# Four graph layers on one core: pair loops written out, and a wait for GpSimd in layer 1

## The chip, the core and the metric

The kernel runs on one core of one Trainium2 chip. The metric is the device time of one execution in microseconds (us). A core has five engines with queues of their own: TensorE (PE; its weight loads are PEld), VectorE (DVE), ScalarE (ACT), GpSimd (POOL) and SyncE (SP), which only issues DMAs here. They meet through semaphores.

## The reference

64 graphs of 128 nodes with 256 features pass through four layers. After each there is a layer norm of x plus the layer's output:

```
x = _layernorm(x + _L0_gnn_ref(x, adj, ...))   # hypergraph convolution, 256 -> 512 -> 256
x = _layernorm(x + _L1_gnn_ref(x, adj, ...))   # attention weights
x = _layernorm(x + _L2_gnn_ref(x, adj, ...))   # three-step random walk
x = _layernorm(x + _L3_gnn_ref(x, adj, ...))   # tanh attention
```

Layer 1, with which much of what follows deals, is

```
q, k = jnp.split(jnp.einsum('bnd,ed->bne', x, W_qk), 2, axis=-1)
v = jnp.einsum('bnd,ed->bne', x, W_v)
scores = jnp.einsum('bnd,bmd->bnm', q, k) * inv_scale
w = jax.nn.softmax(jnp.sum(scores * adj_matrix, axis=-1, keepdims=True), axis=1)
return w * v
```

## The kernel before

Four graphs are a group (GP = 4), so there are 16 groups (G). A layer is a pipeline of steps, one per group; `step(g, p, has)` issues the work of one step on one engine, with p the parity of the buffers and `has(k)` true if group g + k exists. Each engine walks layers 1 to 3 with `over_layers` (L81 on): steps up to 3 are written out with constants, steps 4 to 13 are five passes of a `Fori` over pairs of groups, in which each wait's value and many addresses are computed from a register, and the last steps are written out again, interleaved with the first of the next layer. SyncE's program is already written out (`unrolled=True`). Layer 0 has a loop of its own (`over_groups`) that the change leaves alone. `wait_ge(sem, upto(g, per, k))` waits for k pieces of group g when each group makes `per` of them; `reused(g, back)` is false only for a constant g below `back`.

Numbers are kept as pairs of float16 tiles, hi and lo. `triple` (L105) makes one exact product of three matmuls (L110 to L112). For the next groups x has to be split and transposed:
- ScalarE writes the high half, `x_high` (L1118), two groups ahead.
- GpSimd subtracts to make the low half, `x_low` (L1125): two SBUF inputs, 128x1024, once per group. It waits for the high half and for the buffer.
- SyncE's `transpose_x` (L1139) issues a DMA transpose for each half into xT_hi and xT_lo, high half first, low half when `x_low` is done. Behind it in layer 1 SyncE copies a group of adjT (`stage_adj`, L1181), and comes to the next group's high half.
- TensorE waits for both in `transposed`.

Layer 1, step by step and by engine, in program order:
- TensorE: `aggregate(g-1)` (L1213, fp32), `project(g, 0)` and `(g, 1)` (24 products of 384 columns per group, L110 to L112), `score_rows(g-1)` (L1221, the transpose of the score sums), `project(g, 2)` and `(g, 3)`, `weight_columns(g-1)` (L1225).
- ScalarE: `x_high(g+2)`, `norm_apply(g-2)` four times (L1073), `exponentials(g)` (L1256), `copy_qkv(g+1)` four times (L1250).
- VectorE: `weights(g-1)` (L1282), `residual(g-1)` four times (L1288: l_pre from l_vqk, a column and x_resident, 128x256), two statistics (L1039), `scores(g)` (L1296, L1297, L1302), two statistics, `maximum(g)` (L1306, L1310), `norm_variance(g-1)` (L1046 and on), `softmax(g)` (L1314, L1318).
- GpSimd: `x_low(g+2)`, then `norm_scales(g-1)` (L1058 to L1067), which begins with a wait for the four statistics.

A residual increments the semaphore `L.pre_ok`, four per group. The two loops over the weight columns and the residuals make a cycle: scores of g need the copies of g, the weights need the scores, the residuals the weights.

In layer 2 a TensorE step ends and begins with `walk_mid` (L1513 is its bias matmul), which waits for halves that ScalarE and VectorE have just made from PSUM; `node_scores(g+1)` then waits for xT of group g+1. In layer 3 VectorE's residuals (L1901) read PSUM and SBUF.

Of the kernel before, what the change touches and what calls it, by code (L numbers as in the profile page):

```python
# [12 lines left out]
GP = 4  # L13
# [9 lines left out]
TURNS_PE = ((2, True), (2, True))  # L23
TURNS_ACT = ((2, True), (0, True))
TURNS_DVE = ((2, True), (2, True))
TURNS_POOL = ((2, True), (2, True))
# [11 lines left out]
def upto(g, per, k):  # L38

    return g * per + k  # L40
# [36 lines left out]
def over_layers(eng, programs, turns, unrolled=False):  # L77

    before, drain, after, ahead = None, 0, 2, True
    for (step, lead, lag), (until, next_ahead) in zip(programs, turns + ((2, True),)):
        first = 4 if lag else 2
        for g in range(-2, first):
            for which in ((step, before) if ahead else (before, step)):
                if which is step and g >= -lead:
                    step(g, g % 2, lambda k, g=g: 0 <= g + k < G)
                if which is before and before and G + g + after < G + drain:
                    i = G + g + after  # L90
                    before(i, i % 2, lambda k, i=i: 0 <= i + k < G)
        if not unrolled:
            with eng.Fori(first // 2, G // 2 - 1) as pair:
                step(pair * 2, 0, lambda k: True)
                step(pair * 2 + 1, 1, lambda k: True)
        for g in range(first if unrolled else G - 2, G - 2 + until):
            step(g, g % 2, lambda k, g=g: 0 <= g + k < G)
        before, drain, after, ahead = step, lag, until, next_ahead
    for g in range(G, G + drain):
        before(g, g % 2, lambda k, g=g: g + k < G)  # L100


def reused(g, back=2):

    return not isinstance(g, int) or g >= back  # L105


def triple(nc, out, lhs, rhs, start=True, stop=True, **kw):

    nc.tensor.matmul(out, lhs[0], rhs[1], start=start, stop=False, **kw)  # L110
    nc.tensor.matmul(out, lhs[1], rhs[0], start=False, stop=False, **kw)  # L111
    return nc.tensor.matmul(out, lhs[0], rhs[0], start=False, stop=stop, **kw)  # L112
# [49 lines left out]
def graph_layers(nc, K):  # L162

    with ExitStack() as ctx:
        K.x_new, K.scores_after = {}, {}
        second = layer2(nc, K, ctx)
        with ExitStack() as tiles:
            layers = [layer1(nc, K, ctx, tiles), second]
        layers.append(layer3(nc, K, ctx))
        with nc.Block() as block:  # L170
            @block.sync
            def _(sp):
                over_layers(sp, [sync(sp) for sync, _, _, _, _ in layers], TURNS_SP, unrolled=True)
                sp.wait_ge(K.stored, 16 * (G - 1 + GP))

            @block.tensor
            def _(pe):
                over_layers(pe, [tensor(pe) for _, tensor, _, _, _ in layers], TURNS_PE)

            @block.scalar  # L180
            def _(act):
                over_layers(act, [scalar(act) for _, _, scalar, _, _ in layers], TURNS_ACT)

            @block.vector
            def _(dve):
                over_layers(dve, [vector(dve) for _, _, _, vector, _ in layers], TURNS_DVE)

            @block.gpsimd
            def _(pool):
                over_layers(pool, [gpsimd(pool) for _, _, _, _, gpsimd in layers], TURNS_POOL)  # L190


def setup(nc, K, ctx, W1, b1, gamma, beta, W2, b2, W_qk, W_v, Wv, bv, aw, ab, Wk, bk, w3, a3):
# [900 lines left out]
def front_of(shared, layer):  # L1094
    F = Parts()
    F.x_hi, F.x_lo, F.xT_in, F.xs, F.xT = shared.x_hi, shared.x_lo, shared.xT_in, shared.xs, shared.xT
    F.base = (layer - 1) * G
    F.made = 2
    F.ahead = 2 if layer < 3 else 0
    return F  # L1100
# [7 lines left out]
def x_group(K, g):  # L1108

    return K.x[:, xcols(g - G if isinstance(g, int) and g >= G else g)].rearrange("p (g d) -> p g d", g=GP)  # L1110
# [10 lines left out]
def x_low(K, F, pool, g, p):  # L1121
    pool.wait_ge(F.x_hi, upto(F.base + g, 1, 1))
    if reused(F.base + g):
        transposed(F, pool, g - 2, p)
    pool.tensor_tensor(F.xs[p][1], x_group(K, g), F.xs[p][0], ALU.subtract).then_inc(F.x_lo, 1)  # L1125


def transposed(F, eng, g, p):

    eng.wait_ge(F.xT_in[p], 16 * (F.base + g - p) + 32)  # L1130
# [12 lines left out]
def layer1(nc, K, ctx, tiles):  # L1143
# [10 lines left out]
    L = norm(nc, ctx, "l1", tiles=tiles)  # L1154
# [16 lines left out]
    F = front_of(K.F, 1)  # L1171
# [21 lines left out]
    def tensor(pe):  # L1193
        def project(g, p, j):
            if j == 0:
                transposed(F, pe, g, p)
            if reused(g, 1):
                pe.wait_ge(qkv_sb, upto(g - 1, GP, j + 1))
            for d in range(DT):
                m = triple(nc, b_qkv[j][:, 0:2 * QK + D], [s[:, j, d, :] for s in F.xT[p]],  # L1200
                           [w[:, d, :] for w in K.qkv], start=d == 0, stop=d == DT - 1)
            m.then_inc(qkv_ps, 1)

        def aggregate(g, p):
            pe.wait_ge(a_in[p], 8 * (g - p) + 16)
            pe.wait_ge(qkv_sb, upto(g, GP, GP))
            if isinstance(g, int) and g == 0:
                pe.wait_ge(k_one, 2)
            if reused(g):
                pe.wait_ge(asum_ok, upto(g - 2, 1, 1))  # L1210
                pe.wait_ge(qa_ok, upto(g - 2, 1, 1))
            for j in range(GP):
                m = pe.matmul(b_as[p][:, j * (QK + 1):(j + 1) * (QK + 1)], ast[p][:, j * N:(j + 1) * N],  # L1213
                              vqk[p][:, j, D + QK:D + 2 * QK + 1], start=True, stop=True)
            m.then_inc(ak_ps, 1)

        def score_rows(g, p):
            pe.wait_ge(w_ok, upto(g, 1, 1))
            if reused(g):
                pe.wait_ge(wgt_ok, upto(g - 2, 1, 1))  # L1220
            pe.transpose(b_as[p][0:GP, rows], w[p][:], K.ident[:]).then_inc(wT_ps, 1)  # L1221

        def weight_columns(g, p):
            pe.wait_ge(wn_ok, upto(g, 1, 1))
            pe.matmul(b_as[p][:, cols], wn[p][:], K.ident[0:GP, 0:GP], start=True,  # L1225
                      stop=True).then_inc(wB_ps, 1)

        def step(g, p, has):
            q = 1 - p
            if has(-1):  # L1230
                aggregate(g - 1, q)
            if has(0):
                project(g, p, 0)
                project(g, p, 1)
            if has(-1):
                score_rows(g - 1, q)
            if has(0):
                project(g, p, 2)
                project(g, p, 3)
            if has(-1):  # L1240
                weight_columns(g - 1, q)
        return step, 0, 1

    def scalar(act):
        def copy_qkv(g, p, j):
            act.wait_ge(qkv_ps, upto(g, GP, j + 1))
            if reused(g):
                act.wait_ge(ak_ps, upto(g - 2, 1, 1))
                act.wait_ge(L.pre_ok, upto(g - 2, GP, j + 1))
            act.activation(vqk[p][:, j, 0:D + 2 * QK], b_qkv[j][:, 0:2 * QK + D], ACT.Copy).then_inc(qkv_sb, 1)  # L1250

        def exponentials(g, p):
            act.wait_ge(wneg_ok, upto(g, 1, 1))
            if reused(g):
                act.wait_ge(wn_ok, upto(g - 2, 1, 1))
            act.activation(wexp[p][:], b_as[p][0:GP, rows], ACT.Exp, bias=wneg[p][:], scale=SC,  # L1256
                           accum_out=wsum[p][:]).then_inc(wexp_ok, 1)

        def step(g, p, has):
            q = 1 - p  # L1260
            if halves_due(F, g + 2):
                x_high(K, F, L, act, g + 2, p)
            if has(-2):
                norm_apply(K, L, act, g - 2, p, 0)
                norm_apply(K, L, act, g - 2, p, 1)
                norm_apply(K, L, act, g - 2, p, 2)
                norm_apply(K, L, act, g - 2, p, 3)
            if has(0):
                exponentials(g, p)
            if has(1):  # L1270
                copy_qkv(g + 1, q, 0)
                copy_qkv(g + 1, q, 1)
                copy_qkv(g + 1, q, 2)
                copy_qkv(g + 1, q, 3)
        return step, 2, 2
# [68 lines left out]
        return step, 0, 1  # L1344

    def gpsimd(pool):
        def step(g, p, has):
            q = 1 - p
            if halves_due(F, g + 2):
                x_low(K, F, pool, g + 2, p)  # L1350
            if has(-1):
                norm_scales(K, L, pool, g - 1, q)
        return step, 2, 1
# [611 lines left out]
```

## Time and profile before

| | |
|---|---|
| median of 3 runs | 776.5 us (774.9 to 778.07) |
| the profiled execution | 778.61 us, of which the span of its instructions is 776.8 us |
| TensorE | busy 696.9 us (90%), 5654 matmuls |
| VectorE | busy 588.0 us (76%) |
| ScalarE | busy 531.9 us (68%) |
| GpSimd | busy 343.3 us (44%) |
| mean granted clock of TensorE | 0.948 |
| layer 0, 1, 2, 3 | to about 303, 303 to 446, 446 to 660, 660 to 777 us |
| instruction transfers | 28 of 16 KB on queue q8, 28 of up to 8 KB on q14 |

The profile is one execution. A row of the timeline gives start and duration in us, the engine, the source line, the operation, the tiles that it writes and reads, a count when several are merged (the duration is then from the start of the first to the end of the last), and in brackets the idle time before it with what ended it. A tile's name leaves out buffer numbers. The granted clock is a share of 2.4 GHz.

### The profile page before, as it was taken

Reading aid. Unit: us, or ns where it says so; the run is one execution under the profiler, and the core shown is the slowest. Engines: PE = TensorE matmul, PEld = TensorE weight load, DVE = VectorE, ACT = ScalarE, POOL = GpSimd, SP = SyncE. Lnnn points to the kernel's source line nnn. Section 1 sums busy time; section 2 is a strip of 40 time slices with the busy share of each in tenths; the row PEclk is TensorE's granted clock in tenths of the full one; section 3 lists DMA queues with packets and bytes.
Section 4 is the critical chain, followed back from the end, with each engine's and each line's share of the span. In section 5 each row is a group of like instructions: output and inputs, shape, how many; then the busy total and the mean of one; then the engine's idle time right before and its main releaser. Section 6 shows DMA issues by size and latency. Waiting matters only on the chain.

```text
span 776.8 us, 18723 instructions
## 1 busy us (share of the span) xinstructions
PE 696.9 (90%) x5654; PEld 504.1 (65%) x5654; DVE 588.0 (76%) x1744; ACT 531.9 (68%) x1177; POOL 343.3 (44%) x418
## 2 busy tenths in 40 slices
PE   5899999999999985777878589899989998999995
PEld 5677777777777753444445366566666666888874
DVE  4888888888878762777887876767676876588995
ACT  4668887767777763465555557667776776688885
POOL 2243455434344451444444425243524253677773
PEclk9999999999999997997797689999999999799998
DMA  9522032232221020643444334634343333266663
GB/s 285 154 84 70 29 109 69 73 117 83 68 68 54 2 53 30 149 83 81 95 89 100 55 55 82 83 77 87 81 82 81 81 73 65 55 164 162 162 145 128
DMA packets 168144, 71.11 MB, mean 92 GB/s; under 512 B 122260, under 2 KB 165654, under 8 KB 168088
## 3 DMA queue, kind: packets, MB, share of 16 engines
q1 hardware_dynamic: 166496, 70.41, 37.8%
q8 instruction: 28, 0.46, 0.3%
q10 hardware_dynamic: 1592, 0.01, 0.1%
q14 instruction: 28, 0.23, 0.1%
HBM read 28.46 MB, written 8.39 MB: 47 GB/s over the span
## 4 chain that ended last, share of the span: by engine, by line
PE 39%; DVE 8%; issue 6%; DMA 4%; ACT 2%; SPq 1%; DVEq 1%; POOL 0%; ACTq 0%; POOLq 0%
PE bank L110 10%; PE bank L112 10%; PE bank L111 10%; DMA xT_lo<-x_halves 4%; PE bank L1804 3%; DVE l_pre L1288 2%; DVE l_st L1039 2%; PE bank L1407 2%; PE bank L1802 1%; SPq L1139 1%; PE bank L1225 1%; PE bank L1513 1%; DVE l_w L1302 1%; DVE l_qa L1296 1%; ACT x_resident L1073 1%
## 5 line engine op out<-in xcount | busy, mean ns | idle before, releaser
L1073 ACT ACTIVATE x_resident<-l_pre,l_nmr,l_rstd 128x256 f32 (+1 forms) x256 | 136.9, 595 | 26.8 <-POOL l_nmr L1067 26.7
L1125 POOL TENSOR_TENSOR x_halves<-x_resident,x_halves 128x1024 f16<-128x1024 f16 (+1 forms) x46 | 100.1, 2176 | 39.2 <-ACT x_halves L1118 37.1
L110 PE MATMUL bank<-Wk_lo,xT_hi 128*128 128x2 f16 (+2 forms) x384 | 94.0, 274 | 4.8 <-DMA xT_lo<-x_halves 4.8
L1039 DVE BATCH_NORM_STATS2 l_st<-l_pre 128x6 f32<-128x256 f32 x256 | 96.5, 413 | 1.1
L111 PE MATMUL bank<-Wk_hi,xT_lo 128*128 128x2 f16 (+2 forms) x384 | 95.1, 273 | 0.0
L112 PE MATMUL bank<-Wk_hi,xT_hi 128*128 128x2 f16 (+2 forms) x384 | 94.7, 272 | 0.0
L983 POOL TENSOR_TENSOR hq<-hq 128x512 f32<-128x512 f32 x32 | 43.1, 1347 | 76.6 <-ACT hq L716 76.6
L1064 POOL TENSOR_TENSOR l_rstd<-l_veps,minus_half 128x4 f32<-128x4 f32 x64 | 64.6, 1009 | 24.1 <-DVE l_veps L1053 22.7
L110 PE MATMUL bank<-W2T_lo,h_hi 128*128 128x257 f16 x256 | 70.7, 276 | 2.3 <-DVE h_lo L860 1.2
L111 PE MATMUL bank<-W2T_hi,h_lo 128*128 128x257 f16 x256 | 70.8, 277 | 0.0
L112 PE MATMUL bank<-W2T_hi,h_hi 128*128 128x257 f16 x256 | 70.8, 276 | 0.0
L1729 POOL TENSOR_TENSOR l_T_lo<-l_tf,l_T_hi 128x512 f16<-128x512 f32 x16 | 18.5, 1157 | 106.6 <-ACT l_T_hi L1573 106.6
L860 DVE TENSOR_TENSOR h_lo<-hf,h_hi 128x512 f16<-128x512 f32 x64 | 44.7, 702 | 18.9 <-ACT hf L705 8.3
L1288 DVE SCALAR_TENSOR_TENSOR l_pre<-l_vqk,l_wgt,x_resident 128x256 f32<-128x256 f32 x64 | 55.0, 922 | 1.9 <-DVE l_wgt L1282 1.7
L722 ACT ACTIVATE zf<-bank 128x258 f32<-128x258 f32 x64 | 24.7, 388 | 46.2 <-PE bank L637 46.1
L705 ACT ACTIVATE hf<-bank,b_col 128x512 f32<-128x512 f32 x64 | 44.0, 687 | 16.1 <-PE bank L112 15.6
L110 PE MATMUL bank<-qkvT_lo,xT_hi 128*128 128x384 f16 x128 | 48.0, 375 | 6.2 <-PEq L527 6.2
L110 PE MATMUL bank<-xT_lo,W1T_hi 128*128 128x512 f16 x128 | 48.5, 379 | 1.6 <-DVE qkvT_lo L414 1.5
L112 PE MATMUL bank<-xT_hi,W1T_hi 128*128 128x512 f16 x128 | 48.5, 379 | 0.0
L111 PE MATMUL bank<-xT_hi,W1T_lo 128*128 128x512 f16 x128 | 48.5, 379 | 0.0
L1118 ACT ACTIVATE x_halves<-x_resident 128x1024 f16 (+1 forms) x46 | 48.4, 1052 | 0.0
L971 POOL TENSOR_TENSOR zrs<-zvar,minus_half 128x4 f32<-128x4 f32 x16 | 22.0, 1378 | 59.0 <-DVE zvar L897 59.0
(206 smaller groups left out, 2119.6 us busy)
## 6 DMA issues: line engine op xcount, KB each, us to landing
adj<-in_adj SPq DMA_DIRECT2D x32, 256.0 KB, 3.7
x_halves<-in_x SPq DMA_DIRECT2D x16, 512.0 KB, 3.7
x_resident<-in_x SPq DMA_DIRECT2D x16, 512.0 KB, 4.8
out<-x_resident SPq DMA_DIRECT2D x15, 512.0 KB, 3.2
l_adjT<-adjT_resident SPq DMA_DIRECT2D x16, 256.0 KB, 2.5
x_resident<-in_L_gnn_W SPq DMA_DIRECT2D x2, 512.0 KB, 5.7
x_resident<-in_L_gnn_Wk SPq DMA_DIRECT2D x1, 768.0 KB, 8.1
xT_hi<-x_halves SPq DMA_TRANSPOSE x48, 3.2
```

What stands on the lines that cost most here:

```text
L110: nc.tensor.matmul(out, lhs[0], rhs[1], start=start, stop=False, **kw)
L111: nc.tensor.matmul(out, lhs[1], rhs[0], start=False, stop=False, **kw)
L112: return nc.tensor.matmul(out, lhs[0], rhs[0], start=False, stop=stop, **kw)
L705: act.activation(hf[:, h, :], b_hid[h % 2][:], ACT.Relu, bias=K.b1[:, h:h + 1], scale=1.0 / W_SCALE).then_inc(hf_ok, 1)
L860: dve.tensor_tensor(hs[1][:, h, :], hf[:, h, :], hs[0][:, h, :], ALU.subtract).then_inc(h_lo, 1)
L983: pool.tensor_tensor((hqs if h == HT - 1 else hq[:, 0, :])[:], hq[:, 0, :], hq[:, h, :], ALU.add).then_inc(hqs_ok, 1)
L1039: dve.bn_stats(L.st[p][:, j, :], L.pre[p][:, j, :]).then_inc(L.st_ok, 1)
L1064: pool.tensor_tensor(L.rstd[p][:], L.veps[p][:], K.minus_half[:], ALU.pow).then_inc(L.rstd_ok, 1)
L1073: act.activation(K.x[:, gcols(g, j)], L.pre[p][:, j, :], ACT.Identity, bias=L.nmr[p][:, j:j + 1], scale=L.rstd[p][:, j:j + 1]).then_inc(L. ...
L1118: act.activation(F.xs[p][0], x_group(K, g), ACT.Copy).then_inc(F.x_hi, 1)
L1125: pool.tensor_tensor(F.xs[p][1], x_group(K, g), F.xs[p][0], ALU.subtract).then_inc(F.x_lo, 1)
L1288: dve.scalar_tensor_tensor(L.pre[p][:, j, :], vqk[p][:, j, 0:D], wgt[p][:, j:j + 1], K.x[:, gcols(g, j)], ALU.mult, ALU.add).then_inc(L.pr ...
```

## The change

TensorE, ScalarE, VectorE and GpSimd also get `unrolled=True`: `over_layers` leaves out the `Fori` and calls `step` for every group, in the same order, with constants in all waits and addresses. And in layer 1 GpSimd's low half of group g+2 waits, from the fourth group on, until all four residuals of group g-1 are done. The order of GpSimd's work doesn't change.

```
 def over_layers(eng, programs, turns, unrolled=False):
...
         if not unrolled:
             with eng.Fori(first // 2, G // 2 - 1) as pair:
                 step(pair * 2, 0, lambda k: True)
                 step(pair * 2 + 1, 1, lambda k: True)
         for g in range(first if unrolled else G - 2, G - 2 + until):
             step(g, g % 2, lambda k, g=g: 0 <= g + k < G)
```

```diff
             @block.tensor
             def _(pe):
-                over_layers(pe, [tensor(pe) for _, tensor, _, _, _ in layers], TURNS_PE)
+                over_layers(pe, [tensor(pe) for _, tensor, _, _, _ in layers], TURNS_PE, unrolled=True)
...
             @block.scalar
             def _(act):
-                over_layers(act, [scalar(act) for _, _, scalar, _, _ in layers], TURNS_ACT)
+                over_layers(act, [scalar(act) for _, _, scalar, _, _ in layers], TURNS_ACT, unrolled=True)
...
             @block.vector
             def _(dve):
-                over_layers(dve, [vector(dve) for _, _, _, vector, _ in layers], TURNS_DVE)
+                over_layers(dve, [vector(dve) for _, _, _, vector, _ in layers], TURNS_DVE, unrolled=True)
...
             @block.gpsimd
             def _(pool):
-                over_layers(pool, [gpsimd(pool) for _, _, _, _, gpsimd in layers], TURNS_POOL)
+                over_layers(pool, [gpsimd(pool) for _, _, _, _, gpsimd in layers], TURNS_POOL, unrolled=True)
...
     def gpsimd(pool):
+        def low_half(g, p):
+            if reused(g, 3):
+                pool.wait_ge(L.pre_ok, upto(g - 3, GP, GP))
+            x_low(K, F, pool, g, p)
+
         def step(g, p, has):
             q = 1 - p
             if halves_due(F, g + 2):
-                x_low(K, F, pool, g + 2, p)
+                low_half(g + 2, p)
             if has(-1):
                 norm_scales(K, L, pool, g - 1, q)
```

## Rows read from the trace of the kernel before

**Rows 1.** Windows: start:end, length, busy us per engine, granted clock, DMA share, GB/s.

```profile
302.60:343.90 41.30, 30.78 (x185) 18.85 (x185) 28.10 (x80) 20.63 (x46) 15.63 (x17) 0.95 0.50 112
343.90:439.50 95.60, 76.86 (x373) 45.67 (x373) 74.55 (x215) 54.10 (x121) 41.95 (x55) 0.80 0.39 85
453.10:657.90 204.80, 192.98 (x1700) 132.09 (x1698) 149.09 (x462) 143.97 (x363) 80.49 (x96) 1.00 0.42 80
668.10:770.60 102.50, 99.16 (x1048) 81.76 (x1045) 85.97 (x276) 83.81 (x203) 70.76 (x89) 1.00 0.57 139
```

**Rows 2.** The chain that ended last, in layer 1: start, us, what.

```profile
322.86 0.95 DVE l_pre L1288 x3
324.26 2.10 issue
```

**Rows 3.** VectorE's residuals of layer 1: two groups of the timeline, durations in ns.

```profile
L1288 DVE SCALAR_TENSOR_TENSOR l_pre<-l_vqk,l_wgt,x_resident x64: 472/481/2399, 315.0 to 445.7; 128x256 f32<-128x256 f32 x64
322.86 3.59 DVE L1288 SCALAR_TENSOR_TENSOR l_pre<-l_vqk,l_wgt,x_resident 128x256 f32<-128x256 f32 x4
444.55 1.67 DVE L1288 SCALAR_TENSOR_TENSOR l_pre<-l_vqk,l_wgt,x_resident 128x256 f32<-128x256 f32 x4
```

**Rows 4.** Timeline of a step of layer 1 that is written out already.

```profile
323.11 1.08 PE L1213 MATMUL bank<-l_vqk,l_adjT 128*128 128x65 f32 x8 [0.49 <-issue]
324.04 2.13 POOL L1125 TENSOR_TENSOR x_halves<-x_resident,x_halves 128x1024 f16<-128x1024 f32 x1 [1.10 <-ACT x_halves L1118]
327.94 0.08 PEld L1221 LDWEIGHTS bank<-ident,l_w 128*4 128x4 f32 x1 [2.19 <-DVE l_w L1302]
327.94 0.27 PE L1221 MATMUL bank<-ident,l_w 128*4 128x128 f32 x1 [1.80 <-DVE l_w L1302]
328.83 0.14 DVE L1046 TENSOR_TENSOR l_mdiff<-l_st 128x4 f32<-128x4 f32 x1
330.09 0.38 PE L1225 MATMUL bank<-ident,l_wn 4*128 4x4 f32 x2
330.70 0.88 DVE L1288 SCALAR_TENSOR_TENSOR l_pre<-l_vqk,l_wgt,x_resident 128x256 f32<-128x256 f32 x2
```

**Rows 5.** Timeline of layer 3 under a low half of GpSimd.

```profile
697.01 2.13 POOL L1125 TENSOR_TENSOR x_halves<-x_resident,x_halves 128x1024 f16<-128x1024 f16 x1
697.58 0.74 DVE L1039 BATCH_NORM_STATS2 l_st<-l_pre 128x6 f32<-128x256 f32 x2
698.36 0.81 DVE L1046 TENSOR_TENSOR l_mdiff<-l_st 128x4 f32<-128x4 f32 x1
```

**Rows 6.** Tile xT_lo: in 320:440, in 486.3:492; and TensorE's waits in 455:655.

```profile
L1139 SPq DMA_TRANSPOSE xT_lo<-x_halves x14: 1232/1232/1310, 326.2 to 440.0; - x14
DMA to landing us min/median/max: 3.1/3.1/3.2
...
DMA to landing us min/median/max: 4.7/4.7/4.7
...
PE bank L110 <- DMA xT_lo<-x_halves: 4.8, 4, 1.7
```

**Rows 7.** Timeline of TensorE's bias matmuls in layer 2, first of a step.

```profile
474.10 0.27 PE L1513 MATMUL bank<-bk_parts,ones 128*128 128x256 f16 x1
486.39 0.27 PE L1513 MATMUL bank<-bk_parts,ones 128*128 128x256 f16 x1
...
526.91 0.27 PE L1513 MATMUL bank<-bk_parts,ones 128*128 128x256 f16 x1 [0.36 <-DVE l_mid_lo L1685]
...
551.95 0.27 PE L1513 MATMUL bank<-bk_parts,ones 128*128 128x256 f16 x1 [0.36 <-DVE l_mid_lo L1685]
```

**Rows 8.** DMA queues (packets, MB, share) in 454:518, 518:642 and 668:697.

```profile
q8 instruction: 5, 0.08, 0.6%
...
q8 instruction: 1, 0.02, 0.0%
...
q8 instruction: 2, 0.03, 0.6%
```

## The prediction

> **What bounds the kernel now.** I began with the windows of layers 1 to 3 [rows 1]. In layers 2 and 3 TensorE is busy for 193.0 of 204.8 us and 99.2 of 102.5 us at the full clock, so these layers are TensorE's. Layer 1 is another case: in its first 41.3 us TensorE is busy for 30.8, and from 343.9 to 439.5 the mean granted clock is 0.80. The clock has two levels, 1.0 and 0.5 (2.4 and 1.2 GHz), so 0.80 means that 0.4 of this stretch, 38 us, ran at half clock.
>
> The chain through layer 1 says who sets its step [rows 2]: three residuals of a group on VectorE, then 2.10 us of "issue" before it goes on; behind that it runs through the statistics, the scores, TensorE, and the next group's residuals. The "issue" is explained by the rows of the residual [rows 3]: four instructions take 3.59 us at 322.86, and the single instruction's spread is 472/481/2399 ns. The last group's four, beside which GpSimd has no low half to make, take 1.67 us. At 322.86 GpSimd's subtraction of 2.13 us (the low half of x, group g+2) starts at 324.04, in the middle [rows 4]. One residual per group waits until it ends. The price is 3.59 - 1.67 = 1.92 us a step, on the chain, and TensorE idles for 1.80 us before the transpose of the scores [rows 4].
>
> The first residual starts at 315.0 and the last group's first at 444.55 [rows 3]: 15 steps in 129.5 us, 8.63 each. A step ahead of the loop, at full clock, is 7.84 us (322.86 to 330.70 [rows 3, 4]). So 0.79 us a step goes to register work in the loop and to half clock, and 1.92 us of the rest to GpSimd's subtraction.
>
> **The low half of layer 1 waits for the residuals.** No work is added, one wait per step is. The subtraction of group g+2 now starts behind the fourth residual of group g-1. Set t = 0 at the first residual. The four end at 1.67, so the subtraction runs from about 1.75 to 3.88. What does VectorE do then? Four statistics, the product of scores (one operand in PSUM), a reduction, the maximum (PSUM) and the negation (one tiny operand). The first instruction with two SBUF operands, l_mdiff, starts 2.38 us behind the end of the residuals (328.83 less 326.45 [rows 3, 4]), so at 4.05, when the subtraction is over. Does the subtraction hold what runs meanwhile? Layer 3 shows it: under GpSimd's subtraction from 697.01 to 699.14 two statistics take 0.74 us, which is what two take anywhere, while the l_mdiff behind them lasts 0.81 us instead of 0.14 to 0.16, until the subtraction is over [rows 5]. So I count the hold as gone and not moved: step 7.84 - 1.92 = 5.92.
>
> What comes late next? Two other rings run through the step, and I price each. **TensorE's own ring:** the step of 7.85 us less the wait for the scores, which the weight load puts at 2.19 and the matmul, whose end is modelled late, at 1.80 [rows 4]: 5.66 to 6.05, I take 5.9. In it are a wait of 0.49 for ScalarE's copies ahead of the aggregation and about 0.3 ahead of the weight columns. **The transposed low half:** the subtraction ends at 3.88, SyncE issues at once (the old subtraction ends at 326.17, the issue starts at 326.2), and the data lands 3.1 us later, at 7.0 [rows 4, 6]. The projection of group g+2, one step on, needs it: twelve matmuls stand before the next transpose of scores, some 1.95 us (as many, and the transpose, fit in the 2.15 us from 327.94 to 330.09), and 2.76 us pass from there to the residuals (327.94 to 330.70 [rows 4]). That is 11.7 us for two steps, 5.9 for one. Queued behind the late low half on SyncE are the copy of adjT (issued at 5.1 instead of 4.6, needed a step and more later) and the next high half (due at 6.9, free by 5.8). Behind the new wait on GpSimd stand the norm's scales of group g-1, which wait for statistics that end at 4.0 anyhow. So three rings meet at 5.9 us; nothing has slack, and anything late shows.
>
> On this point the Trainium skill (SBUF — State Buffer, Who interferes with whom) says that a VectorE instruction with at most one SBUF input keeps clear of GpSimd unless it is in a two-port mode, and counts tensor_scalar among those that can enter one. The trace agrees on the statistics; the negation, a tensor_scalar right ahead of l_mdiff, would by that rule be held if the subtraction ran later than I have it. By this count 0.1 us is between them, so the rule gives 0 here, and a few tenths a step if the start slips; the sum doesn't need it.
>
> **The clock.** It fell behind 41.3 us in which TensorE was busy for 75%, with a piece of idling of 1.80 us in every step [rows 1, 4]. With the step at 5.92, 0.8 us of idling is left in pieces of 0.3 to 0.5, a busy share of some 87%; layer 2, at 94%, kept the full clock for 204.8 us. 87 is nearer to 94 and its pieces are short, so I take the clock as full. If it isn't, the 5.1 busy us of a step double; this is a rival below.
>
> **The loops written out.** Gone are 15 loop passes of two groups, with their register arithmetic before waits. In layer 1 this is counted already, since 7.84 is a step ahead of the loop. In layer 2 two written-out steps are 12.29 apart (474.10 to 486.39), two looped ones 25.04 (526.91 to 551.95), 12.52 each, with 0.36 us of idling before walk_mid's bias matmul [rows 7]. Ten steps: 10 x 0.23 = 2.3 us saved. In layer 3 TensorE idles for 3.3 us in all [rows 1]; I take 0.5 saved, with bounds of 0 and 2.
>
> **What is added is code.** The page of DMA queues has a line for instruction transfers: q8 carries 16 KB pages. From 454 to 518 (layer 2, written out) there are five, from 518 to 642 (looped) one; from 668 to 697 (layer 3, written out) two [rows 8]. Does a page cost anything? The transpose of a low half issued at 486.3 shares its flight with one, and lands after 4.7 us instead of 3.1. In layer 2 TensorE waits four times for such a low half, 4.8 us in all, 1.7 at most [rows 6]: three waits of about 1.5, behind 486, 500 and 577, and a small one. Two of the five pages written out hit, and the one of the loop. So: layer 2 gets about 9 more pages, of ten in all two fifths hit, 4 x 1.5 = 6.0, less the 1.5 that the one cost: +4.5. Layer 3 gets 4 to 5 more; transposes are in flight for more than half of its step, but no wait of the kind in layer 2 is in its rows, so I take half and 0.5 each: +1.2. Layer 1 gets 4 more; half hit, at 1.2: +2.4. Bounds: none hits (-1.5, since the one of before may go) and all hit (+1.5 x 18 = +27).
>
> The Trainium skill (Runtime: NRT & Kernel Launch, Instruction fetch mechanics) holds that streaming in straight-line code is mostly hidden and that a taken branch is what breaks it. By that the 8.1 us above would be 0 and the time about 733. The trace shows the other side, the transfer that the page delays; the engine's own fetching cost nothing that I can see.
>
> **Sum**, against the profiled run's 778.6 us (span 776.8):
> - layer 1: 15 x (8.63 - 5.92) = -40.7, pages +2.4: -38.3
> - layer 2: -2.3 + 4.5 = +2.2
> - layer 3: -0.5 + 1.2 = +0.7
> - the turn to layer 2 ran at half clock (439.5 to 453.1) and is bound by dependences; 0, with a bound of -2.
>
> This is -35.4, or 743.2 us. The profiled run lies 2.1 above the median of 776.5, so 741.
>
> **Rivals.**
> - *The clock keeps falling in layer 1.* For: three rings without slack, pieces of idling in each step. Against: busy share nearer to layer 2's. With the old share of half clock (0.4) and a step of 10.2 at half clock (2 x 5.1), the mean step is 1/(0.6/5.92 + 0.4/10.2) = 7.1, layer 1 costs 106.5 instead of 88.8: 741 + 17.7 = 759.
> - *Code pages hit nearly always.* For: transposes are in flight much of every step. Against: two of five. All hits: +27 instead of 8.1, 760.
> - *The hold only moves (the change does not do what it says, and is slower).* GpSimd's subtraction at its new place holds statistics or scores as it held the residual. Then the step stays 8.63 with half clock as before, layer 1 saves the loop's register work alone, 2.3 as in layer 2, and pages cost 2.4 + 4.5 + 1.2 against 2.3 + 0.5: 776.5 - 2.3 + 8.1 - 2.8 = 779.5, and 783.5 when pages hit half again as often: slower. It decides from a hold at the new place of the full 1.9 us a step on. Against it: 0.74 for the two statistics [rows 5].
>
> **Chances.** Forecast (731 to 752) 0.79; clock 0.11; pages 0.06; hold moved 0.04, of which half within 0.5% and half above. The range takes the forecast with bounds: no page hit and the turn at full clock, 731, and on the other side the clock falling in most of the old places, 758. What a measurement can tell here is about 0.5% (3.9 us). Faster 0.96, same 0.02, slower 0.02.
>
> **What would show it.** Four residuals in 1.67 us; the subtraction starting 0.1 us behind them; first residuals 5.9 to 6.1 us apart; granted clock 1.00 from 306 to the end of layer 1; score transpose no longer waiting 1.8 us; q8 pages up from the 28 of the page of before to some 45, and TensorE waiting for xT_lo more often in layer 2. I am wrong if statistics above 0.41 us appear in layer 1, if the step is above 6.5, or if half-clock stretches remain.

## The result

The changed kernel takes 736.5 us (median of 4 runs, 735.6 to 737.1); the kernel before, beside it, 777.3 us. The ratio is 0.947, with a 95% interval of 0.943 to 0.951. Forecast were 741 us, with a range of 731 to 758. Its profiled execution took 737.1 us with a span of 735.2.

In the tables of this document a layer lasts from the first residual of its first group to the first residual of its last group, by the timeline of VectorE; between layers stand the turns.

| us | to layer 1 | layer 1 | turn | layer 2 | turn | layer 3 | end | span |
|---|---|---|---|---|---|---|---|---|
| before | 315.1 | 129.5 | 19.1 | 189.2 | 14.5 | 99.9 | 9.5 | 776.8 |
| after | 316.6 | 90.3 | 18.5 | 186.0 | 11.9 | 102.6 | 9.3 | 735.2 |
| difference | +1.5 | -39.2 | -0.6 | -3.1 | -2.6 | +2.7 | -0.2 | -41.6 |

The 1.5 us ahead of layer 1, where the code is the same, is what two executions differ by; this place was between 313.2 and 316.3 in the runs below.

**Windows of the changed kernel** (start:end, length, busy us per engine with counts, granted clock, DMA share, GB/s): layer 1, 2 and 3.

```profile
308.20:403.80 95.60, 85.45 (x546) 54.73 (x544) 76.62 (x297) 73.00 (x165) 55.43 (x72) 1.00 0.62 129
414.10:615.40 201.30, 193.63 (x1715) 131.65 (x1713) 154.21 (x463) 143.79 (x364) 82.11 (x95) 1.00 0.43 82
618.90:725.00 106.10, 100.64 (x1087) 84.19 (x1085) 73.98 (x270) 87.09 (x211) 72.53 (x89) 1.00 0.59 136
```

Against [rows 1]: the mean clock of layer 1 is 1.00 where 343.9 to 439.5 had 0.80, and TensorE is busy for 85.5 of 95.6 us instead of 76.9, part of which was at half clock. The 15 steps take 90.3 us instead of 129.5; the clock goes to a half at 403.8, in the last 3.0 us of the layer.

**Layer 1's step in the changed kernel**, first the line of the residual (ns: min/median/max), then the timeline (start, us, instruction, and in brackets the idle time ahead and its end).

```profile
L1288 DVE SCALAR_TENSOR_TENSOR l_pre<-l_vqk,l_wgt,x_resident x64: 474/479/486, 316.5 to 408.0; 128x256 f32<-128x256 f32 x64
```

```profile
347.10 1.67 DVE L1288 SCALAR_TENSOR_TENSOR l_pre<-l_vqk,l_wgt,x_resident 128x256 f32<-128x256 f32 x4
347.36 1.08 PE L1213 MATMUL bank<-l_vqk,l_adjT 128*128 128x65 f32 x8 [0.49 <-issue]
348.69 0.75 DVE L1039 BATCH_NORM_STATS2 l_st<-l_pre 128x6 f32<-128x256 f32 x2
348.85 2.13 POOL L1125 TENSOR_TENSOR x_halves<-x_resident,x_halves 128x1024 f16<-128x1024 f32 x1 [1.66 <-DVE l_pre L1288]
349.35 0.41 DVE L1296 TENSOR_TENSOR l_qa<-bank,l_vqk 128x256 f32<-128x256 f32 x1
349.80 0.42 DVE L1302 TENSOR_REDUCE l_w<-l_qa 128x4 f32<-128x256 f32 x1
350.13 0.74 DVE L1039 BATCH_NORM_STATS2 l_st<-l_pre 128x6 f32<-128x256 f32 x2
350.27 0.27 PE L1221 MATMUL bank<-ident,l_w 128*4 128x128 f32 x1
...
351.01 1.23 SPq L1139 DMA_TRANSPOSE xT_lo<-x_halves  x1
351.09 0.14 DVE L1310 TENSOR_SCALAR l_wneg<-l_wmax 4x1 f32<-4x1 f32 x1
351.16 0.14 DVE L1046 TENSOR_TENSOR l_mdiff<-l_st 128x4 f32<-128x4 f32 x1
352.42 0.29 PEld L1225 LDWEIGHTS bank<-ident,l_wn 4*128 4x128 f32 x2 [0.32 <-DVE l_wn L1318]
```

Compare with [rows 3] and [rows 4]. No residual of the 64 is longer than 0.486 us; before, 15 took 2.34 to 2.40. The subtraction starts 0.08 us behind the residuals (GpSimd idled 1.66 us ahead of it, up to l_pre) and ends at 350.98. Beside it lie two statistics of 0.75, the scores, the reduction and two more statistics of 0.74, none longer than without it; the negation comes at 351.09, 0.11 us behind. TensorE's transpose of the scores no longer has a bracket of 1.80. The idling shown is the 0.49 of TensorE and the 0.32 us of its weight load. From here to the next step's first residual (353.04) it is 5.94 us.

**Waits of TensorE in the changed kernel's layer 2** (waiting instruction, releaser, us, times, longest).

```profile
PE bank L110 <- DMA xT_lo<-x_halves: 3.1, 4, 1.3
PE bank L1518 <- ACT l_mid_hi L1572: 1.1, 3, 0.5
```

The same view of its layer 3:

```profile
PE bank L110 <- DMA xT_lo<-x_halves: 4.9, 7, 1.0
```

Before, these waits were 4.8 us in 4 times in layer 2 [rows 6] and 0.5 us in one time in layer 3.

**The DMA queues that carry code, changed kernel** (q8 the 16 KB pages, q14 the 8 KB pages), between the residuals of the first and the last group (packets, MB, share of the 16 engines), layer 2:

```profile
q8 instruction: 13, 0.21, 0.5%
q14 instruction: 12, 0.10, 0.2%
```

and layer 3:

```profile
q8 instruction: 9, 0.15, 0.6%
q14 instruction: 6, 0.05, 0.1%
```

Before, layer 2 had 6 on q8 and 8 on q14, layer 3 had 4 and 3. In the whole kernel q8 went from 28 to 42; forecast were some 45.

### The profile page after: what moved, and what is told of

The parts are those of the page before. It is cut to its first block, busy times and chain, and to the rows that moved or that the text cites. A ratio compares the mean times of both kernels' runs of the same rounds, so it can differ in the third digit from the quotient of the medians.

```text
span 735.2 us, 17541 instructions
## 1 busy us (share of the span) xinstructions
PE 676.4 (92%) x5654; PEld 494.2 (67%) x5654; DVE 554.1 (75%) x1744; ACT 529.9 (72%) x1177; POOL 343.5 (47%) x418
## 4 chain that ended last, share of the span: by engine, by line
PE 36%; DMA 11%; SPq 3%; DVE 3%; issue 2%; POOL 1%; ACT 1%; ACTq 0%; POOLq 0%; DVEq 0%
PE bank L110 11%; DMA xT_lo<-x_halves 11%; PE bank L112 10%; PE bank L111 10%; SPq L1139 3%; PE bank L1213 1%; PE bank L1412 1%; POOL x_halves L1125 1%; DVE l_st L1039 1%; PE bank L1518 1%; DVE l_pre L1288 1%; PE bank L1225 1%; ACT l_mid_hi L1572 0%; DVE l_lr L1652 0%; PE bank L1809 0%
## 5 line engine op out<-in xcount | busy, mean ns | idle before, releaser
L1073 ACT ACTIVATE x_resident<-l_pre,l_nmr,l_rstd 128x256 f32<-128x256 f32 (+1 forms) x256 | 137.1, 598 | 16.6 <-POOL l_nmr L1067 16.6
L1125 POOL TENSOR_TENSOR x_halves<-x_resident,x_halves 128x1024 f16<-128x1024 f32 x46 | 100.9, 2193 | 38.0 <-DVE l_pre L1288 28.0
L110 PE MATMUL bank<-w_lo,xT_hi 128*128 128x1 f16 (+1 forms) x256 | 45.5, 221 | 5.5 <-DMA xT_lo<-x_halves 4.9
L110 PE MATMUL bank<-qkvT_lo,xT_hi 128*128 128x384 f16 x128 | 42.6, 333 | 7.1 <-PEq L527 6.2
L1118 ACT ACTIVATE x_halves<-x_resident 128x1024 f16<-128x1024 f32 x46 | 48.4, 1051 | 0.0
```

The costliest lines, as they stand in the source:

```text
L1073: act.activation(K.x[:, gcols(g, j)], L.pre[p][:, j, :], ACT.Identity, bias=L.nmr[p][:, j:j + 1], scale=L.rstd[p][:, j:j + 1]).then_inc(L. ...
L1118: act.activation(F.xs[p][0], x_group(K, g), ACT.Copy).then_inc(F.x_hi, 1)
```

## Experiments

Each is a small edit of the changed kernel. The times are medians (of 4 executions; 2 for e8, 6 for e11 and e12, 8 for e7), with the ratio to executions of the kernel before made beside them. The layers are those of one profiled execution each.

| kernel | us | ratio (95%) | layer 1 | layer 2 | layer 3 |
|---|---|---|---|---|---|
| e1_unroll_only | 764.3 | 0.982 (0.979 to 0.986) | 117.9 | 190.4 | 101.9 |
| e2_wait_only | 739.3 | 0.952 (0.947 to 0.957) | 92.3 | 189.3 | 98.8 |
| e3_l3_looped | 733.7 | 0.943 (0.939 to 0.946) | 90.1 | 186.4 | 100.1 |
| e4_l3_pe_looped | 732.7 | 0.943 (0.939 to 0.947) | 90.0 | 185.6 | 101.0 |
| e5_wait_three | 735.3 | 0.945 (0.938 to 0.952) | 90.2 | 186.0 | 102.3 |
| e6_wait_two | 745.2 | 0.959 (0.953 to 0.965) | 97.5 | 188.6 | 101.3 |
| e7_unroll_delay | 777.1 | 0.996 (0.992 to 1.000) | 132.1 | 188.6 | 99.3 |
| e8_low_memset | 736.2 | 0.947 (0.938 to 0.956) | 89.2 | 186.3 | 101.6 |
| e9_order | 749.7 | 0.962 (0.958 to 0.966) | 104.6 | 186.7 | 101.5 |
| e10_order_three | 743.8 | 0.958 (0.952 to 0.962) | 95.0 | 188.9 | 102.4 |
| e11_order_l3_pe_looped | 743.1 | 0.953 (0.950 to 0.957) | 98.0 | 188.2 | 100.7 |
| e12_pe_l1_only | 733.6 | 0.946 (0.943 to 0.950) | 90.0 | 185.3 | 100.5 |

### One half of the change at a time

e1_unroll_only drops the wait:

```diff
         def low_half(g, p):
-            if reused(g, 3):
-                pool.wait_ge(L.pre_ok, upto(g - 3, GP, GP))
             x_low(K, F, pool, g, p)
```

> The loops written out, without the new wait. My theory: GpSimd's subtraction holds one residual per step again (four in 3.59 us, the longest single one about 2.4), TensorE idles 1.8 us before the scores' transpose and the clock falls as before. A step of layer 1 at full clock takes 7.84 us, the 15 steps about 127 us instead of 90.3, and the kernel about 772 us. Rival, that writing out is what shortens layer 1: 15 steps near 90 us and a time below 745 us.

In e1_unroll_only, the line of the residual (ns: min/median/max):

```profile
L1288 DVE SCALAR_TENSOR_TENSOR l_pre<-l_vqk,l_wgt,x_resident x64: 478/481/2405, 313.2 to 432.2; 128x256 f32<-128x256 f32 x64
```

Its window of layer 1:

```profile
304.90:427.80 122.90, 86.37 (x545) 54.40 (x543) 104.87 (x297) 73.21 (x165) 56.98 (x72) 1.00 0.48 102
```

The transpose of the scores in its timeline of TensorE:

```profile
341.79 0.27 PE L1221 MATMUL bank<-ident,l_w 128*4 128x128 f32 x1 [1.81 <-DVE l_w L1302]
```

The hold is back (2.405), the step is 7.86 in 11 of the 15 cases, and TensorE idles 1.81 us. But the clock stays full up to 427.8, 3 us before the layer ends: 117.9 us, not the 127 that I expected, and 764.3 us where I expected 772. So writing out alone saves 11.6 us in layer 1, far more than its register work, and the wait then saves 27.6, which is 1.84 a step.

e2_wait_only keeps the wait and takes `unrolled=True` from the four engines:

```diff
-                over_layers(pe, [...], TURNS_PE, unrolled=True)
+                over_layers(pe, [...], TURNS_PE)
```

(and the same for ScalarE, VectorE and GpSimd.)

> The new wait alone, the loops of TensorE, ScalarE, VectorE and GpSimd kept. My theory: four residuals in 1.67 us, written-out steps of layer 1 at 5.93 us, looped ones 0.25 longer (6.2), 15 steps in about 92.5 us, full clock; layers 2 and 3 as in the kernel before (189 and 100 us); the kernel at about 740 us. Rival, that registers in the loop stand in all three rings of layer 1, now that none has slack: looped steps of 6.5 us or more and 744 us or more.

Its window of layer 1:

```profile
306.30:405.30 99.00, 87.45 (x549) 55.65 (x547) 77.33 (x300) 73.40 (x165) 56.44 (x73) 1.00 0.59 125
```

As expected: no residual above 0.486 us, looped steps 6.15 to 6.25 but for one of 6.75 (behind a wait of 0.75 for a low half), 92.3 us in layer 1, full clock in this window. The wait alone gives 38 of the 41 us. The two halves overlap: 11.6 and 37.2 us, but 39.2 together, since with either of them alone the falls of the clock were gone.

### What makes the clock fall

In e1 TensorE idled 1.81 us in each step and was busy for 86.4 of 122.9 us, 70%, and the clock stayed full. The kernel before and e1 differ little up to the first fall: from the clock's rise at 306.3 to its fall at 343.9 TensorE was busy for 27.7 of 37.6 us before, 73.6%, and in the same stretch of e1 (304.9 to 341.6) for 27.1 of 36.7, 73.9%. The fall at 343.9 came in the first looped steps, right behind an idle piece of 2.04 us. e7_unroll_delay puts a fill of 0.22 us a step on the chain of e1, without any loop:

```diff
             if has(0):
+                dve.memset(idle[:], 0.0)      # idle: 128x192, read by nobody
                 scores(g, p)
```

> The loops written out without the new wait, with a fill of 128x192 on VectorE ahead of the scores of layer 1 in each step (0.2 us, an unused tile). Without the fill the step is 7.86 and the clock is full through layer 1, though TensorE idles in one piece of 1.8 us; in the loops of the kernel before, with 2.03, it fell again and again. If the length of that idling tips the clock, the fill brings the falls back: steps of 8.05 at full clock and some of 9 and more, 15 steps of 125 us or above. If it is something in the loop itself, the clock stays full and 15 steps take 121 us.

The fill in its timeline of VectorE:

```profile
356.85 0.22 DVE L1335 MEMSET l_idle<- 128x192 f32 x1
```

Its window of layer 1:

```profile
316.20:448.30 132.10, 102.77 (x509) 61.85 (x510) 107.67 (x316) 70.39 (x158) 56.84 (x75) 0.79 0.43 92
```

The falls are back: mean clock 0.79, steps of 7.97 to 8.07 between others of 9.0 to 9.7, 132.1 us. At full clock a step is 8.03, 0.17 above e1's, so 15 fills add 2.6 us; they cost 14.2 in the profiled executions and 12.8 by the medians of the kernels. (The profiled execution is the slowest of eight; the fastest took 770.9 us, 6.9 above the fastest of e1.) Falls like those of the loop thus come without a loop, from a few tenths of idling more. They began at once: the first three steps are 9.65, 9.59 and 9.08, and the clock fell at 321.5, right behind an idle piece of 2.05 us.

### Is it the reading that holds the residual

e8_low_memset is e1 with another instruction in GpSimd's place (the low half of x is zero in the products of layer 1 and of layer 2's first two groups; the waits of `x_low` are kept):

```diff
-            pool.tensor_tensor(F.xs[p][1], x_group(K, g), F.xs[p][0], ALU.subtract).then_inc(F.x_lo, 1)
+            pool.memset(F.xs[p][1], 0.0).then_inc(F.x_lo, 1)
```

> The loops written out without the new wait; GpSimd fills the low half of x with zeros in layer 1 instead of subtracting, so the low part of x is missing in the products of layer 1 and of the first two groups of layer 2. The fill starts where the subtraction did, amid the residuals, but reads nothing from SBUF. If the hold comes from the reading of two engines, no residual is held: 0.48 us each, and the step is 5.9 us without the new wait; the low half is also ready over 2 us sooner, so if the step is still 5.9, the ring through the transposes isn't what sets it. Rival, that any work of GpSimd holds the residual: the step is 7.86 less what the fill is shorter.

Its timeline of VectorE and, in the second fence, of GpSimd in one step:

```profile
332.06 1.67 DVE L1288 SCALAR_TENSOR_TENSOR l_pre<-l_vqk,l_wgt,x_resident 128x256 f32<-128x256 f32 x4
```

```profile
333.23 0.95 POOL L1351 MEMSET x_halves<- 128x1024 f16 x1 [1.07 <-ACT x_halves L1118]
```

The fill starts in the midst of the residuals, 0.03 us ahead of the fourth, where e1's subtraction started 0.01 ahead of it, and the four take 1.67 us all the same. So it is not GpSimd's being at work, but its reading from SBUF while VectorE wants two operands from there. The step is 5.94, though the low half is ready 1.8 us sooner than in the changed kernel (2.12 instead of 3.88 us behind the first residual): the ring through the transposes does not set the 5.93.

e6_wait_two and e5_wait_three change the count that is waited for (to 2, and to 3 in e5_wait_three):

```diff
-                pool.wait_ge(L.pre_ok, upto(g - 3, GP, GP))
+                pool.wait_ge(L.pre_ok, upto(g - 3, GP, 2))
```

> The changed kernel, with the low half waiting for two of the four residuals. If the hold comes from the shared way to SBUF and is decided by who starts first, the third residual is on its way and the fourth is held until the subtraction ends: one residual of about 2.0 to 2.4 us per step, a step of 7.5 to 7.9 us, the kernel at 760 to 764 us, like without the wait. Rival, that the start of the subtraction and not the overlap matters: 5.93 us and 736.

> The changed kernel, with the low half waiting for three of the four residuals. It asks what sets the step of 5.93 us. The subtraction can start some 0.4 us earlier, beside the fourth residual. If GpSimd then waits until the fourth is done, or the fourth has read already, nothing is held and the ring through the transposed low half is shorter by up to 0.2 us a step: if that ring sets the step, it falls to 5.75 and the kernel to 733.5 us; if TensorE's or VectorE's ring does, it stays 5.93 and 736. Rival: the fourth residual is held like in the kernel before (2.4 us), the step is near 7.8 and the kernel near 764.

Two steps of e6_wait_two, in the timelines of VectorE (residuals) and, in the second fence, of GpSimd (subtractions):

```profile
333.76 1.67 DVE L1288 SCALAR_TENSOR_TENSOR l_pre<-l_vqk,l_wgt,x_resident 128x256 f32<-128x256 f32 x4
342.24 3.55 DVE L1288 SCALAR_TENSOR_TENSOR l_pre<-l_vqk,l_wgt,x_resident 128x256 f32<-128x256 f32 x4
```

```profile
335.00 2.42 POOL L1125 TENSOR_TENSOR x_halves<-x_resident,x_halves 128x1024 f16<-128x1024 f32 x1 [1.16 <-DVE l_pre L1288]
343.30 2.21 POOL L1125 TENSOR_TENSOR x_halves<-x_resident,x_halves 128x1024 f16<-128x1024 f32 x1 [1.16 <-DVE l_pre L1288]
```

The fourth residual by itself in these two steps:

```profile
334.95 0.48 DVE L1288 SCALAR_TENSOR_TENSOR l_pre<-l_vqk,l_wgt,x_resident 128x256 f32<-128x256 f32 x1
343.43 2.36 DVE L1288 SCALAR_TENSOR_TENSOR l_pre<-l_vqk,l_wgt,x_resident 128x256 f32<-128x256 f32 x1
```

I expected a hold in every step or in none. It came in three of 15, each a step of 7.81, and which it is goes by who starts first. In these three the subtraction starts 0.13 to 0.14 us ahead of the fourth residual (343.30 against 343.43), and the residual lasts 2.35 to 2.36 us. In the other twelve it starts 0.04 to 0.05 us behind it (335.00 against 334.95), the residual takes its 0.48, and the subtraction lasts 2.42 to 2.43 instead of 2.13: now GpSimd is the one that waits. Where the two started within 0.01 us of each other, as in most steps of e1, it was always the residual that was held. The wait for two is not what sets the subtraction's start, though the bracket names the residual: ScalarE's high half ends 0.13 to 0.14 us ahead of it in all 15 steps, and the second residual ended before that. The step of 8.48 us, the one between the two shown, has no hold: TensorE waited 0.73 us for a low half in it, and the clock was at a half from 336.1 to 339.5.

With three, GpSimd's span was 2.30 to 2.31 in all steps and no residual was held; undisturbed steps stayed at 5.93 to 5.94, as expected if the rings of TensorE and VectorE set them. The wait for all four keeps the residuals clear of the subtraction wherever ScalarE's work ends, and costs nothing.

### Can the step be made shorter

e9_order shortens the rings of TensorE and VectorE in layer 1 (VectorE's part in short):

```diff
             if has(0):
                 project(g, p, 0)
+            if has(-1):
+                aggregate(g - 1, q)            # was ahead of project(g, p, 0)
+            if has(0):
                 project(g, p, 1)
...
-            stats 0, 1; scores(g); stats 2, 3; maximum(g); norm_variance(g - 1); softmax(g)
+            scores(g); stats 0, 1; maximum(g); stats 2, 3; softmax(g); norm_variance(g - 1)
```

> The changed kernel with another order in layer 1: TensorE aggregates behind the first projection (it no longer waits 0.49 us for ScalarE's copies), VectorE makes the scores ahead of the statistics, the maximum behind two of them, the softmax ahead of the variance. The rings of TensorE and VectorE get shorter, to about 5.45 and 5.5 us by the rows. If these set the step of 5.93, it falls to what the ring through the transposed low half allows, which I put at 5.87 (two steps in 11.7): 15 steps in 88 to 89 us, the kernel at 734 to 735. Rival, that something shorter binds in neither: 5.5 us a step and 730.

One projection in its timeline of TensorE:

```profile
345.64 0.39 PE L110 MATMUL bank<-qkvT_lo,xT_hi 128*128 128x384 f16 x1 [1.90 <-DMA xT_lo<-x_halves]
```

TensorE's waits in its layer 1:

```profile
PE bank L110 <- DMA xT_lo<-x_halves: 13.7, 7, 2.7
```

Windows of its layer 1, and of the stretch from the clock's rise to its first fall:

```profile
315.70:420.30 104.60, 87.74 (x513) 56.48 (x514) 77.07 (x301) 70.91 (x158) 57.71 (x74) 0.89 0.52 116
308.20:318.50 10.30, 8.76 (x58) 5.70 (x57) 3.56 (x12) 5.22 (x11) 3.15 (x2) 1.00 0.45 106
```

It is 13 us slower than the changed kernel, where 1.5 to 2.5 us less were expected. Every second group TensorE waits 1.9 us for the low half, and steps alternate, 5.42 and 8.9, or 5.42 and 7.4 in the two pairs in which the clock stayed full. The two short rings reach 5.42, so they, one or both, had set the 5.93. The third ring spans two steps, and I had moved the aggregation and the scores into it: they now stand behind the projection that waits for the transposes. The sum of two steps is 12.8 at full clock, not 11.7. The rest of the loss goes with the clock: 23.3 us of the layer ran at half clock, against 3.0 in the changed kernel. It first fell at 318.5, after 10.3 us in which TensorE was busy for 85%, and 1.5 us behind an idle piece of 1.54 us.

e10_order_three adds the wait for three, e11_order_l3_pe_looped also TensorE's loop in layer 3:

> The same order, with the low half waiting for three residuals. With three the subtraction of the low half ended 0.2 to 0.3 us earlier, and the ring through it spans two steps: a step 0.1 to 0.15 below that of the kernel with the order alone, about 5.75 us, 15 steps in 87 us, the kernel at 733 to 734, if that ring binds there; no difference if it does not. A risk: subtraction and fourth residual start closer together, and a held residual costs 1.9 us in its step.

> The order and the wait for three, and TensorE's loop kept in layer 3 (five q8 pages fewer there). If the gains add up: layer 1 in 87 us and layer 3 in 100 to 101 us, the kernel at 730 to 731 us. If pages in layer 3 do not matter, it is that of the same kernel with layer 3 written out.

In e10 two steps are 7.04 and 5.5, 12.6 together, 0.12 a step below e9's 12.8 at full clock: that the low half comes a little earlier does count, as expected, because in this order that ring binds. But that is about 2 of the 9.6 us between 104.6 and 95.0. The rest goes with the clock: 3.9 us of e10's layer 1 ran at half clock and 23.3 of e9's. e11 has the same code in layer 1 as e10, with 10.3 us at half clock and 98.0 us. The level of 87 us was off for both, and so were the times: neither is under 90.3 in layer 1, and layer 3's gain (100.7) doesn't make up for it.

### What the written-out code costs

e3_l3_looped keeps the `Fori` in layer 3 on all four engines, e4_l3_pe_looped on TensorE alone (SyncE is written out everywhere, as before):

```diff
-        for g in range(first if unrolled else G - 2, G - 2 + until):
+        for g in range(first if written else G - 2, G - 2 + until):   # written: per layer
...
-                over_layers(pe, [...], TURNS_PE, unrolled=True)
+                over_layers(pe, [...], TURNS_PE, unrolled=(True, True, False))
```

> The changed kernel with layer 3 in its loop again on all four engines. My theory: layer 3 lost 2.7 us by being written out (99.9 to 102.6 us from the first to the last group's residuals), because pages of code delay its transposes; looped, it is back at about 100 us and the kernel at 734 us, with one or two q8 pages in layer 3 instead of eight. Rival, that the loss is not from pages but from another timing of the engines at the start of the layer: layer 3 stays at 102 us or more, the kernel at 736.5.

> The changed kernel with layer 3 in its loop again on TensorE alone. If the 16 KB pages of queue q8 are TensorE's and these are what delays the transposes, q8 has no page in the looped stretch and layer 3 takes about 100 us, as with all four engines looped (734 us). If the 8 KB pages of the other engines count as much, layer 3 stays between 101 and 102.6 us and the kernel at 735.5 us or more.

TensorE's waits in layer 3 of e3_l3_looped, which the changed kernel has at 4.9 us in 7 times:

```profile
PE bank L112 <- DMA xT_lo<-x_halves: 1.0, 3, 0.5
```

The queues that carry code there:

```profile
q8 instruction: 4, 0.07, 0.2%
q14 instruction: 3, 0.02, 0.1%
```

and in layer 3 of e4_l3_pe_looped:

```profile
q8 instruction: 4, 0.07, 0.3%
q14 instruction: 6, 0.05, 0.1%
```

So q8 carries TensorE's pages and q14 those of other engines: TensorE's loop alone takes q8 from 9 to 4 and leaves q14 at 6. Layer 3 took 99.9, 98.8, 100.1 and 100.5 us with all loops (before, e2, e3, e12); 101.0 and 100.7 with TensorE's alone (e4, e11), written out between 99.3 and 102.6 in eight kernels, 101.6 on average. So writing out layer 3 costs about 2 us, of which TensorE's program (nine pages instead of four) is about half. e3 came out as expected, but for four q8 pages instead of one or two; e4 lies between its two expectations (101.0 us, but 732.7). That a page delays a transpose shows in the landings: in the changed kernel, of the low halves' transposes from layer 1 on, all 28 with no page in their flight landed in 3.0 to 3.2 us, those with 8 KB pages took up to 4.1 and those with a 16 KB page up to 4.5. How much of layer 3's 2 us that is, is less sure: written-out kernels lie between 99.3 and 102.6, so the halves are no more than a reading.

e12_pe_l1_only asks the same of layer 2: loops on all engines in layer 3, and on TensorE alone in layer 2.

> The changed kernel, with layer 3 looped on all four engines and layer 2 looped on TensorE alone. It asks what writing out gives in layer 2, where loops cost 0.2 us a step and pages of code delay transposes. If the 0.2 us are the registers of VectorE and ScalarE and the late low halves come from TensorE's pages, layer 2 (first to last group's residuals) takes 184 us or less instead of 186, and the kernel 731 to 732. If the 0.2 us are TensorE's registers, layer 2 gets 2 us back from pages and loses 2: 186 us and 733.5, like with layer 3 alone looped. If pages cost nothing, layer 2 takes 188 to 189 us and the kernel 735 to 736.

Layer 2 takes 185.3 us, against 185.6 to 186.4 in the changed kernel, e3 and e4. Its steps are 12.2 to 12.4 where none is disturbed, like written out, with TensorE's program looped. So the 0.2 us a step came from the loops of the other engines; that it is their registers is argued, not shown. q8 has 6 pages instead of 13, and TensorE still waits 2.3 us in four times for the low half, against 3.1: TensorE's pages are less than half of the disturbance in layer 2, by one execution of each. It ends at 733.6 (731.8 to 739.7). None of the three expectations fits whole: the time is that of the second, the steps are those of the first, and layer 2 lies between them.

e3, e4 and e12 lie 3 to 4 us below the changed kernel, by medians 733.7, 732.7 and 733.6 against 736.5. Their intervals overlap with its own, so a version that keeps the loops of layer 3 is likely a little better, and not shown to be.

## Why the prediction was right, and where it wasn't

- **The hold goes and isn't moved.** Priced at 1.92 us a step from [rows 3]; 7.84 to 5.93 is 1.91. The reading of [rows 5], that statistics pass under a subtraction and l_mdiff doesn't, held for every instruction in the step. e8 shows the cause, and e6 that the order of the starts decides who waits. What the Trainium skill (SBUF — State Buffer, Who interferes with whom) says about two SBUF inputs against a reading GpSimd agrees with the traces: 0.48 beside a fill, 2.4 beside a subtraction. Its warning on tensor_scalar had nothing to bite on; the negation starts 0.11 us behind the end of the subtraction, and no run here puts the two together.
- **The step.** Forecast 5.92, measured 5.93 to 5.94 in 12 of 15. I had three rings at 5.9. e8 shows that the third has room (a low half 1.8 us earlier changes nothing), and e9 that TensorE's and VectorE's had set it (with both shortened, steps of 5.42 occur); which of the two it is stays open. It was right that TensorE's rows gave 5.66 to 6.05. The count of the third ring was right only for the order that the kernel had.
- **Layer 1** -39.2, forecast -38.3. Pages cost 0.9 and 0.3 us in two steps (6.81 and 6.28), 1.2 instead of 2.4. The first of them was not a page of q8: the low half issued at 332.3 landed after 4.1 us, with two pages of q14 in its flight. I had priced TensorE's pages alone (four more, it was two) and left those of the other engines out.

The queues in that flight, 332.0 to 336.4 of the changed kernel, and its transpose with the us to landing:

```profile
q14 instruction: 2, 0.02, 1.7%
...
xT_lo<-x_halves SPq DMA_TRANSPOSE x1, 4.1
```

- **The clock.** It was full, as forecast, but the reason I gave fell, and to that extent the forecast was luck. I held the busy share (a forecast 87% against 75%; it was 89%) and the piece of 1.80 us responsible. The 75% were read over a stretch that began at half clock; at full clock it was 73.6%, and e1, at 73.9% in the same stretch and 70% over the layer, with pieces of 1.81, keeps the full clock. e9 and e11 lose it at 85 and 86%, so 87% alone promised nothing. What I counted as -12 from clock and registers together would have come from writing out alone, as it did in e1 (-11.6). In these kernels TensorE idled at each fall of layer 1 or shortly ahead of it, mostly for more than 1.5 us (0.73 us in e6), but as long pieces passed without a fall too. Why 7.86 stands and 8.03 falls is open; the runs only show where it happens.
- **Layer 2** -3.1, forecast +2.2: the failed step is the term of pages. I took two hits in five from 64 us and 1.5 us each, so +4.5. TensorE's waits for a low half were 3.1 us after, and 4.8 before: with more than twice the q8 pages (13 for 6; forecast 15) the loss went down, not up. I had named more such waits in layer 2 as a sign; there were four, as before. In e1 the same code had 1.5, 1.7 and 1.8, and layer 2 took 190.4. Which page meets which transpose changes from run to run, and the clock has a part: the written-out kernels whose layer 2 kept the full clock took 185.6 to 186.7 us, and the five with one fall of 3.4 us (e1, e6, e7, e10, e11), each behind a wait of 1.5 to 1.7 us for a low half, took 188.2 to 190.4. The registers, 2.3 forecast, are the difference between undisturbed steps, 12.5 and 12.2 to 12.3. By the Trainium skill (Runtime: NRT & Kernel Launch, Instruction fetch mechanics) pages would be free and the time 733; the measured 736.5 lies between that and my 741, and e3 at 733.7 shows that some of the cost is there.
- **Layer 3** +2.7, forecast +0.7. Here the hits were more than I took, 7 waits with 4.9 us.
- **The turn to layer 3** -2.6, which I hadn't priced: it ran 10.2 us at half clock before and 3.4 us after. In the other kernels this turn was 11.7 to 13.7 us, with none to 6.8 us at half clock, in step with it.

Against the 743.2 us that the sum gave for a profiled run, this one, 737.1, came 6.1 us lower. By terms: layer 1 -0.9, layer 2 -5.3, layer 3 +2.0, the two turns -3.2, and 1.3 the other way outside of all of them. So layer 1 carried the result, and what is off lies in the pages of layer 2 and in the turn.

## What to carry to other kernels

A long maximum beside a short median in one instruction's durations, at the same place in each step, is worth a look at what GpSimd reads at that time; moving a subtraction by 0.6 us, from 1.19 to 1.75 us behind the first of four instructions with two SBUF operands, so that it stood behind all four and beside instructions with one such operand or with PSUM, gave 28 to 37 us here, with no work removed. When several rings through a step have nearly the same length, shortening two of them by moving work into the third makes it slower: write down what each ring contains after the move. And before the price of a small delay is taken as its length, look whether the engine behind it sits near a fall of its clock.

## What was not expected of the hardware

- A fill on VectorE that made a step 0.17 us longer, 2.6 us in all, cost 14.2 us, since TensorE's clock fell in layer 1 (117.9 to 132.1 us; mean clock 1.00 to 0.79). The busy share of TensorE doesn't tell which side a kernel is on: e1 kept the full clock at 70%, e9 lost it at 85%. The same code can do either: layer 1 of e10 kept it for 85 us, that of e11 lost it after 48.
- When a subtraction of GpSimd and a residual start at about the same time, the one that starts first runs and the other waits: 0.13 us ahead the subtraction held the residual (2.36 instead of 0.48 us), 0.04 us behind it was itself longer (2.42 instead of 2.13).
- A transpose of a low half that shared its flight with two 8 KB pages landed after 4.1 us instead of 3.1; with one of 16 KB, before the change, after 4.7.
